# Second attention with one head per 64 rows: scores and maxima as pairs of matmuls in one ring of three bank pairs

## What is computed

```python
xq = jnp.einsum('bsh,oh->bso', x, wq).reshape(B, S, nh, hd)   # the same for xk, xv; nh 16, hd 16
xq, xk = _apply_rope(xq, cos, sin), _apply_rope(xk, cos, sin)
scores = jnp.einsum('bqhd,bkhd->bhqk', xq, xk) / np.sqrt(hd)
probs = jax.nn.softmax(scores, axis=-1)
out = jnp.einsum('bhqk,bkhd->bqhd', probs, xv).reshape(B, S, nh * hd)
return jnp.einsum('bso,ho->bsh', out, wo)
```

## Time and profile before

| what | value |
|---|---|
| median of the runs | 2819.57 us (2819.38 to 2823.9) |
| the profiled execution's own time | 2827.23 us |
| its span | 2825.4 us |
| mean granted clock | 0.958 of 2.4 GHz |

### The profile page before, as it was taken

One profiled execution on the slowest core, in us unless ns is written; L12 is line 12 of the kernel. 1 busy time (PEld: TensorE's weight loads), 2 busy tenths in 40 slices (PEclk: granted clock), 3 DMA queues, 4 the chain that ended last, 5 costly groups with the idle time before them and its releaser, 6 DMA issues. The chain is left out here.

```text
span 2825.4 us, 35427 instructions
## 1 busy us (share of the span) xinstructions
PE 2586.7 (92%) x13494; PEld 1666.8 (59%) x13494; DVE 1858.8 (66%) x2874; ACT 1452.8 (51%) x1903; POOL 910.7 (32%) x553
## 2 busy tenths in 40 slices
PE   5989989989995999999999949999999999999699
PEld 3444545545553778888888834555555555554488
DVE  5776676676652644555454458887888888787454
ACT  2434434434441546666766614566566566666443
POOL 0654655655663324444443421110010011000144
PEclk7999999999997999999999967999999999999899
DMA  1000100100002400000000043343333433231222
GB/s 37 24 9 14 38 24 16 39 24 16 24 26 90 142 1 23 23 23 23 23 1 23 15 113 61 68 88 60 64 70 56 77 79 61 52 54 23 81 83 75
DMA packets 118622, 130.07 MB, mean 46 GB/s; under 512 B 21424, under 2 KB 92592, under 8 KB 118448
## 3 DMA queue, kind: packets, MB, share of 16 engines
q1 hardware_dynamic: 118448, 127.73, 19.3%
HBM read 93.21 MB, written 33.69 MB: 45 GB/s over the span
## 5 line engine op out<-in xcount | busy, mean ns | idle before, releaser
L1884 DVE TENSOR_REDUCE c_mraw<-c_X 128x1 f32<-128x512 f32 x1024 | 651.7, 685 | 124.5 <-PE c_X L105 116.2
L1806 ACT ACTIVATE c_P<-c_S 128x1024 f32<-128x1024 f32 x512 | 495.8, 1020 | 244.9 <-PE c_S L105 241.2
L105 PE MATMUL c_X<-c_K,c_Q 96*128 96x512 f32 x1024 | 368.7, 443 | 11.9 <-DMA c_Q<-bounce_q 7.0
L461 ACT ACTIVATE a_P<-a_S 128x1024 f32<-128x1024 f32 x256 | 249.0, 1023 | 251.3 <-PE a_S L105 251.3
L105 PEld LDWEIGHTS c_X<-c_K,c_Q 96*128 96x128 f32 x1024 | 181.7, 193 | 265.4 <-issue 194.9
L569 DVE TENSOR_REDUCE a_mraw<-a_X 128x2 f32<-128x1024 f32 x170 | 207.6, 1221 | 148.9 <-PE a_X L105 148.8
L105 PE MATMUL c_S<-c_Q,c_K 98*128 98x512 f32 x1024 | 287.6, 402 | 1.8 <-DMA c_Q<-c_mrow 1.7
L105 PE MATMUL c_O<-c_P,c_V 128*32 128x512 f32 x2048 | 273.6, 606 | 0.2 <-ACT c_P L1806 0.2
L688 POOL TENSOR_TENSOR a_accp<-a_accp,a_P 128x1024 f32<-128x1024 f32 x96 | 252.8, 2634 | 62.5 <-ACT a_P L461 54.4
L1159 POOL TENSOR_TENSOR b_act0l<-b_xf,b_act0h 128x512 fp32r<-128x512 f32 x128 | 170.1, 1330 | 295.1 <-ACT b_act0h L1024 295.1
L105 PE MATMUL a_O<-a_P,a_V 128*64 128x512 f32 x1024 | 259.5, 630 | 0.0
(11 more groups left out here) (301 smaller groups left out, 5474.6 us busy)
## 6 DMA issues: line engine op xcount, KB each, us to landing
c_K<-bounce_k SPq DMA_DIRECT2D x64, 256.0 KB, 7.4
c_Q<-bounce_q SPq DMA_DIRECT2D x128, 128.0 KB, 4.7
a_rinv<-sums SPq DMA_DIRECT2D x64, 128.0 KB, 2.9
b_h_w<-in_L_ffn_h_w SPq DMA_DIRECT2D x16, 512.0 KB, 6.3
bounce_k<-c_comp SPq DMA_DIRECT2D x16, 512.0 KB, 3.3
bounce_q<-c_comp SPq DMA_DIRECT2D x16, 512.0 KB, 3.0
a_ln_x<-in_L_attn_x SPq DMA_DIRECT2D x4, 1024.0 KB, 6.3
a_xres<-in_L_attn_x SPq DMA_DIRECT2D x32, 128.0 KB, 2.6
```

The costliest lines, as they stand in the source:

```text
L105: return pe.eng.matmul(out, lhsT, rhs, start=start, stop=stop, skip_group_check=True)
L461: act.eng.activation(P[n % NP][:, :, :], psS[n % 2][:, :, :], ACT.Exp, scale=SCALE).then_inc(s_exp)
L1806: act.eng.activation(P[n % NP][:, 2 * hp:2 * hp + 2, :], psS[hp][:, :, :], ACT.Exp, scale=SCALE).then_inc(s_exp)
L1884: dve.eng.tensor_reduce(mraw[u % 2][:, at:at + 1], psX[X.slot(key)][:, :], AX.X, ALU.max).then_inc(X.free(key))
```

## The change

Each head gets 64 rows of its own: 16 each of high, low, high for Q and high, high, low for K (48 rows), the maximum as row 48 in a single fp32r part, and filling. Two heads lie over each other in the 128 partitions and two side by side. A matmul of the scores (64 rows) or the maxima (48 rows) for head 0 of a pair is followed at once by that for head 1 in the other 64 rows, into the other bank of a pair of banks. One ring `R` of three pairs of banks serves scores and maxima, in the written order of `pair_order`; DVE reduces two banks in one instruction. Everything else has a single bank `X`. LEAD is 12. The cosine product and both low parts move to POOL, with a copy of the bank by ACT ahead of them. Fetches are six DMAs of 128 KB (K) and 64 KB (Q). The last banks of output use the ring of pairs.

```diff
-    NH, NG, NP, LEAD = 4, 4, 2, 10
+    NH, NG, NP, LEAD = 4, 4, 2, 12
-    TAIL = [(B - 1, t) for t in range(2, NT)]
+    TAIL = [(B - 1, t) for t in range(4, NT)]
+    QUERY_PARTS, KEY_PARTS = (0, 1, 0), (0, 0, 1)
...
-        if t not in (2, 5):
+        if t not in (2, 6):
...
+    def rows_at(u, t):
+        return u + 1 if t == 5 and u + 1 < NU else None
+    def finish_at(u, t):
+        return u - 1 if t == 3 and u else None
...
-        return project_at(*divmod(n - 2, NT)) if n >= 2 else None
+        return project_at(*divmod(n - 3, NT)) if n >= 3 else None
...
+    def pair_order():
+        out = [("max", k) for k in range(2 * LEAD)]
+        for n in range(STEPS):
+            for i in range(2):
+                out += [("scores", n, i)]
+                out += [("max", 2 * (n + LEAD) + i)] if n + LEAD < STEPS else []
...
-        psS = [p.ps(f"S{i}", [128, 2, 512]) for i in range(2)]
-        psO = p.ps("O", [128, 512])
-        psX = [p.ps(f"X{i}", [128, 512]) for i in range(3)]
-        X = Ring(p, "x", 3, x_order())
+        psR = [p.ps(f"R{i}", [128, 2, 512]) for i in range(3)]
+        psO, psX = p.ps("O", [128, 512]), [p.ps("X", [128, 512])]
+        X = Ring(p, "x", 1, x_order())
+        R = Ring(p, "pair", 3, pair_order())
...
+            def fetch(tile, src, sem):
+                for i, part in enumerate(src):
+                    heads = part.rearrange("(i h r) n -> h r i n", i=2, h=2)
+                    for h in range(2):
+                        rows = slice(64 * h + 16 * i, 64 * h + 16 * i + 16)
+                        sp.eng.dma_start(f32(tile[rows, :, :]), heads[h]).then_inc(sem, 16)
...
+            def keep_projection(key):
+                i, x = nth[key], ("project", *key)
+                act.wait_ge(*X.filled(x))
+                if i >= 2:
+                    act.wait_ge(s_rot, 3 * (i - 2) + 1)
+                act.eng.activation(qk[i % 2][:, :], psX[0][:, :], ACT.Copy).then_inc(s_qk)
...
                 act.eng.activation(osp[t % 2][0][:, :, :], src, ACT.Copy).then_inc(s_oh)
+                if i >= 2:
+                    act.wait_ge(s_ol, i - 1)
+                act.eng.activation(osr[t % 2][:, :, :], src, ACT.Copy).then_inc(ring.free(key))
...
-            dve.eng.memset(f32(KT[0][64:98, :, :]), 1.0).then_inc(s_fill)
-            for i in range(2):
-                dve.eng.memset(f32(QT[i][64:96, :, :]), 0.0).then_inc(s_fill)
+            for tiles, value in ((KT, 1.0), (QT, 0.0)):
+                for tile in tiles:
+                    for h in range(2):
+                        dve.eng.memset(f32(tile[64 * h + 32:64 * h + 64, :, :]), value).then_inc(s_fill)
...
+                dve.eng.tensor_reduce(mraw[u % 2][:, at, :], pair(key)[:, :, :], AX.X, ALU.max).then_inc(R.free(key))
...
+                pool.eng.tensor_tensor(t1[i % 2][:, :], qk[i % 2][:, :], rope[0][:, cols], ALU.mult).then_inc(s_rot)
+                pool.wait_ge(*X.emptied(("project", *key)))
                 pool.eng.tensor_tensor(t2[i % 2][:, :], t2[i % 2][:, :], rope[1][:, cols], ALU.mult).then_inc(s_rot)
...
-            for key in EARLY:
+            for i, key in enumerate(EARLY):
                 rotate(key)
+                send_low(key)
...
+                for h in range(2):
+                    rows = slice(64 * h, 64 * h + 48)
+                    ins = mm(pe, pair(key)[:, h, :], QT[u % 3][rows, i, 128 * q:128 * q + 128], KT[u // 2 % 2][rows, i, 512 * kh:512 * kh + 512])
+                ins.then_inc(R.full(key))
...
+                for h in range(2):
+                    rows = slice(64 * h, 64 * h + 64)
+                    ins = mm(pe, pair(key)[:, h, :], KT[u // 2 % 2][rows, i, 128 * t:128 * t + 128], QT[u % 3][rows, i, :])
+                ins.then_inc(R.full(key))
...
             for n, (u, t) in enumerate(steps()):
-                scores(n)
-                if n + LEAD < STEPS:
-                    for i in range(2):
-                        maxima(n + LEAD, i)
+                for i in range(2):
+                    scores(n, i)
+                    if n + LEAD < STEPS:
+                        maxima(2 * (n + LEAD) + i)
+                if pending:
+                    project_out(*pending)
+                pending = out_at(u, t)
                 if n >= 1:
                     weigh(n - 1)
```

More of the change, by code:

```diff
@@ L1577, in x_order @@
         out = [("turn", 0, i % 2, i // 2) for i in range(4)]
[L1578 to L1581, removed]
+        out += [("project", *e) for e in EARLY] + [("values", 0, t) for t in range(NT)] + [("rows", 0)]
         pending = None
[L1583 to L1586, removed]
+        for u, t in steps():
             out += [("out", *pending)] if pending else []
             pending = out_at(u, t)
+            out += [("finish", finish_at(u, t))] if finish_at(u, t) is not None else []
+            out += [("rows", rows_at(u, t))] if rows_at(u, t) else []
             out += [("turn", *turn_at(u, t))] if turn_at(u, t) else []
-            if u >= UB or not project_at(u, t) or project_at(u, t)[0]:
-                out += [("project", *project_at(u, t))] if project_at(u, t) else []
+            out += [("project", *project_at(u, t))] if project_at(u, t) else []
             out += [("values", *values_at(u, t))] if values_at(u, t) else []
             out += [("back", *pending)] if pending else []
[L1594 to L1601, removed]
+        return out + [("out", *pending), ("finish", NU - 1)]
+    def pair_order():
[4 more added lines that the diff above has]
+                out += [("max", 2 * (n + LEAD) + i)] if n + LEAD < STEPS else []
+        for i, x in enumerate(TAIL):
+            out += [("last_back", *x)]
+            out += [("last_out", *TAIL[i - 1])] if i else []
+        return out + [("last_out", *TAIL[-1])]
     with ExitStack() as ctx:
@@ L1652, in unit, with pair @@
             return b, r // 2, r % 2
+        def pair(key):
+            return psR[R.slot(key)]
         def sent(key):
@@ L1670, in finished, with back_bank, out_bank, projected @@
             return ("finish", UB * b + 6 + half)
+        def back_bank(b, t):
+            key = ("last_back" if (b, t) in TAIL else "back", b, t)
+            return (R, key, pair(key)[:, 0, :]) if (b, t) in TAIL else (X, key, psX[0][:, :])
+        def out_bank(b, t):
+            key = ("last_out" if (b, t) in TAIL else "out", b, t)
+            return (R, key, pair(key)[:, 0, :]) if (b, t) in TAIL else (X, key, psX[0][:, :])
+        def projected(b, t):
+            ring, key, _ = out_bank(b, t)
+            return ring.filled(key)
         def sync(eng):
@@ L1724, in store @@
                 i = out_index(b, t)
-                sp.wait_ge(*X.emptied(("out", b, t)))
+                ring, key, _ = out_bank(b, t)
+                sp.wait_ge(*ring.emptied(key))
                 sp.eng.dma_start(x_tiles(x_out, b)[:, t, :], xres[i % 4][:, :]).then_inc(s_store[i % 4], 16)
@@ L1872, in send_low @@
[L1872 to L1888 removed]
+                    dve.wait_ge(s_rot, 3 * (i - 2) + 3)
@@ new lines, in swap, with reduce @@
+                dve.eng.stream_shuffle(t2[i % 2][:, :], psX[0][:, :], PAIRS).then_inc(X.free(x))
+            def reduce(k):
+                u, at, key = k // 16, k % 16, ("max", k)
+                if at == 0 and u >= 2:
+                    dve.wait_ge(s_max, u - 1)
+                dve.wait_ge(*R.filled(key))
+                dve.eng.tensor_reduce(mraw[u % 2][:, at, :], pair(key)[:, :, :], AX.X, ALU.max).then_inc(R.free(key))
+                if at == 15:
+                    for j in range(3):
+                        dve.wait_ge(*R.emptied(("max", k - j)))
@@ L1906, in finish @@
                 if b:
-                    dve.wait_ge(*X.filled(("back", b - 1, 4 * half + 3)))
+                    ring, back, _ = back_bank(b - 1, 4 * half + 3)
+                    dve.wait_ge(*ring.filled(back))
                 out = TON[:, 4 * half:4 * half + 4, 64 * g:64 * g + 64].rearrange("p q (h d) -> p q h d", h=NH)
@@ L2040, in weigh @@
                 b, g, _ = unit(u)
-                pe.wait_ge(s_exp, 2 * n + 2)
+                for i in range(2):
+                    pe.wait_ge(*R.emptied(("scores", n, i)))
                 pe.wait_ge(*X.emptied(("values", b, t)))
@@ L2106, in tensor @@
                 pending = out_at(u, t)
+                if n >= 1:
+                    weigh(n - 1)
+                if finish_at(u, t) is not None:
+                    finish(finish_at(u, t))
+                if rows_at(u, t):
+                    max_rows(rows_at(u, t))
                 if turn_at(u, t):
                     norm.turn_pe(pe, *turn_at(u, t), ident[:, :])
-                if project_at(u, t) and project_at(u, t)[0]:
+                if project_at(u, t):
                     project(project_at(u, t))
```

296 lines of the change are left out of this document (131 added, 165 removed).

## The result

The changed kernel takes **2878.67 us** (median of 4, 2876.26 to 2889.63) against 2819.48 of the kernel before: ratio 1.021, 95% interval 1.0185 to 1.0243. The forecast was 2864, range 2836 to 2892. The profiled execution after took 2876.37 (span 2874.2). It is only 49 over the profiled one of before, because the first two stages, which the change doesn't touch, ran 11.8 us shorter in it (the second attention starts at 1625.2 instead of 1637.0). From that stage's first instruction to the next stage's first it is 1011.0 before and 1071.3 after: **+60.3**, which agrees with the medians. I compare by that stretch from here on.

What follows compares the result with a forecast made beforehand. The prediction took PE's throughput to bound the kernel's step. Loop +18, ahead of it +24 and behind it +3 gave +45 us: 2872 profiled, with the median 7.7 under it, so 2864 us, range 2836 to 2892.

Steps and rivals of the forecast that it cites:

- The plain step: Loop step without extra work, S0, M0, S1, M1 (S scores, M maxima), then weighing: 3.05 us, 3.06 before.
- the circle: Plain step: S0 to exponential 0.55, exponential 1.02, to M1 0.05, M1 to weighing 0.43, weighing 1.00; sum 3.05.
- rival 5: Pairs of matmuls don't run at once with 48 rows: +119 us, 2983; chance 0.03.
- Plain units: Loop units of eight plain steps: finish and max row cost 0.4 instead of 0.74, 24.8 each, -12 in all.
- Projections: In the loop: 1.7 each against 1.54, with ACT's copy ahead of the next exponential; +4 over 28.
- Outputs: In the loop: 2.05 each against 1.30, with ACT's copies and waits for single bank X; +18 over 24.
- Prologue: Ahead of the loop, all serial: fillings +8.2, turns +6.8, early projections +12.0, smaller fetch -3.2; together +23.8.
- what ends last is the first fetch: Ahead of the loop: PE idles for the first fetch, which ends last; its smaller size gives -3.2.
- Rival 1: DVE's reductions bound the loop's step at 2.44; 244 steps save 0.61 each, -149, 2715 us; chance 0.04.
- Rival 2: Cheaper restarts of PE in the loop: step 2.85, -51 us, 2813; chance 0.06.
- Rival 3: A fetch arrives late in the loop, Q behind a send: 14 units late by 2 us, +28, 2892; chance 0.10.
- Rival 4: The clock stays low in the loop: 4.2 instead of 3.05 over 256 steps, +294 us, 3158; chance 0.05.

Runs made afterwards that it cites:

- p1: The changed kernel with the exponential of the first scores taking 256 of 512 queries, part of the work left out: 2776.8 us (one run).
- p2: The changed kernel with every reduction of the maxima reading 256 of 512 keys of each bank: 2868.7 us (one run).
- e3: The changed kernel with the ten fillings moved between the four early swaps and the early low parts back on DVE: 2876.8 us, 1.022.
- e2b: The changed kernel with the weighing as two halves, one right after the other where the whole one was: 2887.7 us, 1.026.
- c2b: The changed kernel with early turns, projections and values in the ring of pairs, fillings moved, early low parts on DVE: 2866.4 us, 1.015.
- e2f: The changed kernel with the weighing halved, between first maxima and second scores and after second maxima, start flag on first half only: 2799.9 us, 0.993.
- c3: The changed kernel with the halved weighing of e2f and the part ahead of the loop of c2b: 2772.9 us, 0.983.
- c4: c3 with the maxima 11 instead of 12 steps ahead (LEAD 11): 2765.6 us, 0.980.
- q1: The changed kernel with the normalization's scaling of eight tiles in the loop spread over four steps instead of two: 2890.0 us, 1.025.

## Why the prediction was right, and where it was not

Right in sign and range, with its mechanism; 14.7 us too low. The stretch of the stage took 60.3 more where the sum had 45: +36 for +18 in the loop, and the rest nearly as forecast.

- **The plain step**: 3.05 forecast, 3.05 measured, with each of the five terms, PE idle 0.65 ahead of M1 (0.8 forecast), DVE idle 0.61 a step (3.05 less twice 1.22). p1 and p2 show the circle from both sides. The Trainium skill (TensorEngine Tiling (Array Packing), PSUM Bottleneck) warns of the readers; here one reader's latency bounds the step by the ring's order, and by the rule as a bound of throughput it would be 2.44, which no run reached: 2.62 with halves.
- **Pairs at once** (rival 5): they do, at 48 rows too.
- **Plain units**, -12 forecast, 0 measured (27 to 29: 25.2 each). The step with a finish takes 3.63: its four transposes begin 0.99 after the weighing's start and hold the next S0 up by 0.59, and the max row costs 0.16 more. I had 0.4 for both; they cost 0.75, as before. This step of the sum failed by 12 us.
- **Projections**: 1.64 each (3.28 for two above a plain unit); forecast 1.7. Right.
- **Outputs**: a clean unit with three (unit 25 in e3) takes 30.77, so 1.86 each; forecast 2.05. The eight units with outputs or values took 20.3 more than before, 6.1 of it low clock; the forecast had +18 for outputs and +8 for turns and values.
- **Normalization and low clock**: this step of the sum was missing. Units 0, 1, 2, 9, 10, 17 and 18, where the next batch is normalized and turned, took 18.3 more than before. Across the four runs with the same loop (after, e2b, e3, c2b), the changed kernel's steps sum to 10.6 over the fastest of the same steps, 9.2 of it in six steps at the low clock, and that is a lower bound, since unit 1 was low in all. The turns stood in the +8; the normalization beside them and the low clock stood nowhere. The forecast had +2 for the clock, at the loop's beginning alone.
- The loop by units: those with projections +0.8, plain ones -1.3, outputs and values 20.3, normalization 18.3, last two units -2.1 (forecast -2): **+36 for +18 forecast**.
- **Prologue**: +22.2 to the first maxima and +1.6 in them, for 23.8. The fillings +7.4 (8.2), the turns +6.9 (6.8), the four early projections +10.7 (12.0). The smaller fetch: from the end of the last low part to its landing 12.3 for 15.8, -3.5 (-3.2). The step "what ends last is the first fetch" failed, but cheaply: the values, which the sum didn't have, ended 0.7 behind it. That the whole comes out at 23.8, as forecast, is luck in the tenths: errors of under 2 us of both signs cancel.
- **Tail**: +0.3 for +3.
- **Rival 1** (DVE): refuted by p2. **Rival 2** (2.85): no restart was cheaper. **Rival 3** (fetch late): not in the changed kernel, where PE waits for no DMA in the loop, but in e2f and c3, whose steps are shorter; c4 cured it. **Rival 4** (clock stays low): not as written, 1.00 in the windows of most units, but a piece of it is true. The Trainium skill (TensorE: Matmul & The Clock Gate, What's actually happening) says that the low state is the default and activity releases it. The traces agree in so far as the fall at 1778.38 comes after PE was busy 1.75 of 4.00 us, and no such fall is in the loop before, where PE was busy 900 of 914.6.

Why the clock falls in some steps and not in others of the same kind stays open: e3 and the changed kernel have the same loop, and the low stretches lie in different steps of units 9 to 25. c3 against c2b (the same prologue; two against twelve stretches) speaks for PE's idle time as the cause, but e2f, as busy as c3, has six, and no run varied the idle time alone. One long wait is not the cause of all of them, as the four falls without one show; whether it is that of unit 1's stays open.

## What to carry to other kernels

When two kinds of work share one ring of banks and one in-order engine fills it, walk the circle from one fill through its reader to the next use of that bank and count everything that stands behind the waiting instruction; halving the engine's own work does nothing while that sum stays. The cure is to split the largest instruction group that has no bank of its own, and to put its pieces where the waits are (here 3.05 to 2.62); moved as a whole it only joins another circle (3.25). Work left to a single bank becomes serial: here four turns cost 6.9 us more than in three banks, and eight values at 2.12 each caught up with the fetch. Before one of two chains is called the one that ends last, look when the other ended: here 1 us before. And an engine that now waits may lose its clock: here at least 9 us.

## What the runs showed of the hardware

- **DVE was held up by POOL.** The four scalings at 1773.43 took 3.33 us; alone they take 1.37 (0.407 each is the median of 32). POOL's additions and multiplications stood at 1772.10, 1773.34 and 1774.69, and the two scalings beside the last two took 1.33 and 1.43. In q1 two scalings beside POOL's operations took as much, and PE's wait stayed. In the kernel before no scaling in this attention took over 0.412. The Trainium skill (SBUF — State Buffer, SBUF: two separate sides) says that the two engines share a pair of ports, which one holds for a whole instruction; the trace fits that, with the delay about one POOL operation. The change moved two operations of each projection to POOL without a cost for DVE in my sum.
- **A matmul of half the columns costs a little over half.** The eight of a weighing, of 512 columns, take 0.99 from start to next start; eight of 256 take 0.56 and 0.57. So sixteen small ones cost 0.14 more.
